# Unread identity matmuls in three waits of TensorE, and a constant in place of a computed wait before expert 0's later tiles

## The reference

```python
h = layernorm(x) * (1 + ca) + sa
xn = rms_scale * h / (norm(h) * D**-0.5 + 1e-8) * split_scale
K = sigmoid(xn @ W_K)
u, g_in, g_out = split(xn @ W_ugg, 3)
u = u * sigmoid(g_in) * (1 - K)
outputs = scan(a * prev + b, a=Kshift, b=u)        # along the sequence
x = x + ga * (outputs * sigmoid(g_out) @ W_out + h)
h = layernorm(x) * (1 + cb) + sb
# each token goes to 2 of 8 experts, with weights w
x = x + gb * sum_e w_e * (gelu(h @ W1[e] + b1[e]) @ W2[e] + b2[e])
```

## Time and profile before

| what | value |
|---|---|
| time, median of 3 runs | 755.43 us (754.45 to 755.51) |
| profiled execution: span, first to last instruction | 770.2 us |
| its time over the span | not given apart from the span |
| TensorE busy | 705.5 us, 92% of the span |
| VectorE, ScalarE, POOL busy | 517.6, 416.1, 393.3 us |
| mean granted TensorE clock | 0.956 of full speed |
| opening, up to the first main product | 24.15 us |
| main stage | last logits of group 6 at 288.3 us |
| expert stage, from its first product | 312.24 us |

### The profile page before, as it was taken

One profiled execution on the slowest core, in us unless ns is written; L12 is line 12 of the kernel. 1 busy time (PEld: TensorE's weight loads), 2 busy tenths in 40 slices (PEclk: granted clock), 3 DMA queues, 4 the chain that ended last, 5 costly groups with the idle time before them and its releaser, 6 DMA issues.

```text
span 770.2 us, 16815 instructions
## 1 busy us (share of the span) xinstructions
PE 705.5 (92%) x4854; PEld 651.0 (85%) x4854; DVE 517.6 (67%) x1788; ACT 416.1 (54%) x1082; POOL 393.3 (51%) x309
## 2 busy tenths in 40 slices
PE   5899999999999993489998999999998999999991
PEld 1678888788888873389998999999898999999991
DVE  5878879998887668375553754647866476476451
ACT  5456564655546351165654755547665575475560
POOL 1264637785683654633534635446555445463443
PEclk9799999999999995589999999999999999999996
DMA  8441012230110413414457344555553553433432
GB/s 300 146 160 56 1 55 71 83 112 29 56 55 31 153 69 106 152 40 73 62 111 175 61 73 64 121 132 166 124 114 63 123 130 91 100 62 63 74 70 37
DMA packets 50308, 72.54 MB, mean 94 GB/s; under 512 B 5808, under 2 KB 42108, under 8 KB 50240
## 3 DMA queue, kind: packets, MB, share of 16 engines
q0 software_dynamic: 16480, 27.28, 19.4%
q1 hardware_dynamic: 33760, 44.46, 18.4%
HBM read 48.85 MB, written 22.87 MB: 93 GB/s over the span
## 4 chain that ended last, share of the span: by engine, by line
PE 76%; DVE 9%; issue 6%; DMA 4%; ACT 2%; POOL 2%; SPq 0%; DVEq 0%; another core or an unknown queue 0%; POOLq 0%; ACTq 0%
PE mm L965 24%; PE yb L976 23%; PE mm L810 17%; PE yb L835 5%; PE tp L944 2%; DMA out_x<-ysb,tokb 2%; PE tp L866 1%; PE tp L825 1%; PE tp L853 1%; DVE hl L1330 1%; ACT xnb L651 1%; DMA mb<-mod_rows 1%; DMA gbr<-mod_rows,xm 1%; DVE bst L1011 1%; DMA h2all<-in_L_wmod 1%
## 5 line engine op out<-in xcount | busy, mean ns | idle before, releaser
L783 ACT ACTIVATE hh<-mm,b1T 128x256 fp32r<-128x256 f32 (+1 forms) x288 | 135.9, 472 | 174.5 <-PE mm L965 124.5
L576 POOL DMA_INDIRECT out_x<-ysb,tokb x68 | 109.2, 1606 | 187.2 <-DVE ysb L1359 147.0
L1330 DVE TENSOR_TENSOR hl<-mm,hh 128x256 fp32r<-128x256 f32 (+1 forms) x288 | 116.3, 407 | 128.5 <-ACT mm L784 115.3
L965 PE MATMUL mm<-fh,SH 128*128 128x256 f32 x576 | 166.4, 289 | 22.7 <-DVE hl L1330 8.4
L965 PE MATMUL mm<-fl,SH 128*128 128x256 f32 x576 | 163.3, 283 | 0.0
L965 PE MATMUL mm<-fh,SL 128*128 128x256 f32 x576 | 162.9, 283 | 0.0
L976 PE MATMUL yb<-SH,hh 128*128 128x256 f32 x544 | 156.9, 288 | 0.0
L976 PE MATMUL yb<-SH,hl 128*128 128x256 f32 x544 | 153.6, 282 | 0.0
L976 PE MATMUL yb<-SL,hh 128*128 128x256 f32 x544 | 153.5, 282 | 0.0
L965 PEld LDWEIGHTS mm<-fh,SH 128*128 128x128 f32 x576 | 110.7, 192 | 26.5 <-DVE hl L1330 10.3
L784 ACT ACTIVATE mm<-mm,b1T 128x256 f32<-128x256 f32 (+1 forms) x288 | 127.5, 443 | 0.0
(11 more groups left out here) (218 smaller groups left out, 1172.8 us busy)
## 6 DMA issues: line engine op xcount, KB each, us to landing
xin<-disp_x SPq DMA_DIRECT2D x74, 132.0 KB
wraw<-in_L_ffn_W SPq DMA_DIRECT2D x8, 1024.0 KB
h2all<-in_L_ffn_W SPq DMA_DIRECT2D x8, 1024.0 KB
xb<-in_L_attn_x SPq DMA_DIRECT2D x8, 512.0 KB, 7.5
out_x<-x2b SPq DMA_DIRECT2D x8, 512.0 KB
mb<-mod_rows SPq DMA_DIRECT2D x3, 768.0 KB, 6.4
wraw<-in_L_attn_W_ugg SPq DMA_DIRECT2D x1, 1536.0 KB, 10.2
gbr<-mod_rows,xm POOLq DMA_INDIRECT x74
```

Of the source, the lines that this page charges most:

```text
L576: e.indirect_dma_start(out=out_rows, out_offset=bass.IndirectOffsetOnAxis(ap=tokb[:, j:j + 1], axis=0), in_=ysb[:, j, :], in_offset=None, ...
L783: e.activation(hh[:, f, c_], mm[f % 4][:, c_], ACT.Gelu_apprx_tanh, bias=bias)
L965: i = e.matmul(mm[f % 4][:, 0:TE], a[:, k, f * 128:(f + 1) * 128], b[:, k, :], start=(k == 0 and t == 0), stop=(k == 1 and t == 2))
L1330: e.tensor_tensor(hl[:, f, w_], mm[f % 4][:, w_], hh[:, f, w_].bitcast(F32), ALU.subtract)\
```

## The change

TensorE's program gets a helper, `keep_busy(n)`: n matmuls of `ident` by `ident` (128 by 128, fp32) into 128 columns of `yb[1]`, which nobody reads. Six are issued as soon as `ident` is made, three after the transpose of `vrow`, 28 after the mod products and before the transposes of group 0. On ScalarE `ln1_square(0)` moves ahead of `mod_rows(0)`. On SP `wait_for_groups` and the registers that it uses are taken out; in its place SP waits for `SENT_8` once, between expert 0's first tile and its later ones, and the wait for `SENT_8` behind those tiles goes.

```diff
--- before.py
+++ after.py
@@ -359,12 +359,9 @@
                 for j in range(2):
                     e.dma_start(xin[:, j, :], rows_of(j)).then_inc(S["rows_loaded"], 16)
 
-            r_late, r_soon, r_sooner, r_sent = (e.alloc_register("sp_" + k) for k in ("late", "soon", "sooner", "sent"))
+            r_late = e.alloc_register("sp_late")
             e.wait_ge(S["late_ready"], 1)
             e.reg_load(r_late, lateint[0:1, 0:1])
-            e.reg_load(r_soon, lateint[0:1, 1:2])
-            e.reg_alu(r_soon, r_soon, 1, ALU.logical_shift_left)
-            e.reg_add(r_sooner, r_soon, 1)
             e.reg_mov(r_last, CAP - 128)
             e.wait_ge(S["sent0"], 16 * 8 * 4)
             e.wait_ge(S["sent1"], SENT_6)
@@ -388,22 +385,7 @@
                     e.reg_add(r_pos, r_pos, 128)
                     return Xd[bass.ds(e.snap(r_at, min_val=0, max_val=E * CAP - 128), 128), :]
 
-                def wait_for_groups():
-
-                    e.reg_add(r_sent, r_pos, TE)
-                    e.reg_alu(r_sent, r_sent, 1, ALU.logical_shift_left)
-                    e.reg_alu(r_sent, r_sent, r_soon, ALU.max)
-                    e.reg_alu(r_sent, r_sent, r_sooner, ALU.min)
-                    e.reg_alu(r_sent, r_sent, 1, ALU.bitwise_and)
-                    e.reg_alu(r_sent, r_sent, 8, ALU.logical_shift_left)
-                    e.reg_add(r_sent, r_sent, SENT_6)
-                    e.reg_alu(r_sent, r_sent, SENT_6, ALU.max)
-                    e.wait_ge(S["sent1"], r_sent)
-                    e.sem_inc(S["tick_sp"], 1)
-
                 def tile(first, parts):
-                    if n == 0 and not first:
-                        wait_for_groups()
                     load(rows_of)
                     if first and n == 0:
                         e.wait_ge(S["x2_scaled"], NG)
@@ -420,8 +402,8 @@
                 if n == 0:
                     tile(True, 2)
                     ks = counts_of(e)
+                    e.wait_ge(S["sent1"], SENT_8)
                     more_tiles(e, ks, n, tile)
-                    e.wait_ge(S["sent1"], SENT_8)
                     load_b2(1, E)
                 else:
                     tiles(e, ks, n, tile)
@@ -711,8 +693,8 @@
             ln1_scale(0)
             weights_high(0, 0)
             weights_high(0, 1)
+            ln1_square(0)
             mod_rows(0)
-            ln1_square(0)
             weights_high(1, 0)
             weights_high(1, 1)
             ln1_xn(0)
@@ -883,9 +865,16 @@
                 e.matmul(o, ones[:, :], bc(csum[:, :], 4), start=False, stop=True,
                          skip_group_check=True).then_inc(S["ranked"], 1)
 
+            def keep_busy(n):
+
+                for _ in range(n):
+                    e.matmul(yb[1][:, 0:128], ident[:, :], ident[:, :], start=True, stop=True)
+
             e.wait_ge(S["const_made"], 6)
+            keep_busy(6)
             e.wait_ge(S["vec_loaded"], 64)
             e.transpose(tp[0][:, 0:76], vrow[:, :], ident[0:76, 0:76]).then_inc(S["vec_turned"], 1)
+            keep_busy(3)
             e.wait_ge(S["c_silu"], 1)
             e.wait_ge(S["wmod_loaded"], 16)
             for to, c0 in ((mm[3], D), (yb[0], 0)):
@@ -900,6 +889,7 @@
                     i = e.matmul(mm[n][0:NB, :], scT[:, k, :], wmod_sb[:, k, n * 512:(n + 1) * 512],
                                  start=(k == 0), stop=(k == 1))
                 i.then_inc(S["mod_made"], 1)
+            keep_busy(28)
             turn_xn(0)
             for g in range(NG):
                 last = g == NG - 1
```

## The result

The changed kernel takes 758.84 us (median of 14 runs), the kernel before 755.30 in runs beside it: a ratio of 1.0045, interval 1.0029 to 1.0060. It is slower by 0.45%, 3.4 us. The forecast was 755.0, no change, in a range up to 757.5.

The account below looks back on a forecast made before the run. TensorE was taken to bound the kernel, but group 1's normalized rows, behind the mod-row chain, to gate the opening. Opening -0.4 us, constant wait 0: 755.4 - 0.4 = 755.0 us, range 752.6 to 757.5.

Parts of the forecast that it names:

- the constant wait: 0: SP's load of expert 0's second tile: wait over by 327.8 at worst, 8 us before the need; cost 0.
- Rival E: Expert 0's second tile: needed at 328.4, its rows arrive 324.5 to 330.8; 0 to 2.4 us lost; chance 0.10.
- the 0.58 for no change: Whole kernel: the chance given to a measured time within 0.2% of the kernel before.
- The opening: Up to group 1: the guards' chain starts 0.4 us earlier and everything behind group 1 moves with it; -0.4 us.
- keep_busy(6) and (3): Opening, TensorE: 12 passes of 2.6 us and 6 of 1.3 us fit before DMA waits end; cost nothing.
- the 56 passes: keep_busy(28) behind the mod products: 0.116 us each, 6.5 us in all, from 14.4 to 20.9.
- The block's overrun: keep_busy(28) ends at 20.9, the rows to be turned are ready at 20.77: overrun 0.1 us.
- Rival C: Opening: clock rises late, keep_busy(28) ends at 23.7, group 0's transposes start 2.9 us late; 757.6; chance 0.16.
- Rivals B: Opening: mod-row chain shorter in timed runs, so TensorE gates and its saved 2.7 us go through; 752.3; chance 0.18.
- D: New TensorE idle before 49.5: clock falls, 3.25 us at the lower level cost 1.6 us; 756.6; chance 0.08.
- one time for the rise: Opening: TensorE's clock reaches its upper level near 7.9, as work begins at 2.1 and 5.8 us precede the rise.

Follow-up runs that it names:

- e1: Kernel before, its computed wait written as a branch around a constant wait; old opening: 754.94 us, ratio 1.0005 to the kernel before.
- e2: e1 plus the change's lines on TensorE and ScalarE (new opening, computed wait): 755.45 us, ratio 1.0001 to the kernel before.
- e3: Kernel before with only the change's SP lines (constant wait ahead of tile 2, old opening): 758.50 us, ratio 1.0061.
- e4: As e3, but the constant wait stands behind the load of each later tile of expert 0: 756.09 us, ratio 1.0016 to the kernel before.
- e5: e1 with the first gating of W_out moved from POOL to VectorE behind its first scan: 755.62 us, ratio 1.0017 to the kernel before.
- e9: e1 (old opening, computed wait) with POOL's first gather of gate rows ahead of its last four sends: 752.38 us, ratio 0.9956 to the kernel before.
- e6: e2 with the first gating of W_out moved from POOL to VectorE behind its first scan: 757.27 us, ratio 1.0030 to the kernel before.
- e8: Changed kernel (constant wait) with POOL's first gather of gate rows ahead of its last four sends: 760.08 us, ratio 1.0090 to the kernel before.
- e7: e2 with POOL's first gather of gate rows ahead of its last four sends: 751.29 us, ratio 0.9966 to the kernel before.
- e11: e7 with 14 instead of 28 idle matmuls ahead of group 0's transposes: 752.37 us, ratio 0.9970 to the kernel before.
- e12: e7 with 44 instead of 28 idle matmuls ahead of group 0's transposes: 756.01 us, ratio 1.0016 to the kernel before.
- e10: e9 with only the swap of squares and mod_rows on ScalarE: 751.72 us, ratio 0.9963 to the kernel before.

## Why the prediction was wrong

**The step that failed** is "the constant wait: 0". It took the need for tile 2's rows from one row, 335.89, and SP's present issue from another, 327.62, and found 8 us of slack. Both rows came from an execution that had been held up by 14 us between tiles 1 and 2. Without that, the need is at 318 to 319 and the issue at 313.5 to 313.9 (e1, e2). The release of the wait was well bounded (0 to 6.4 us after POOL's last send; measured 2.9, and SP's load followed at 322.03). Set against a need at 318, it gives a wait of TensorE of 3 us at the least; measured were 7.6, since the load takes 3.5 more from its issue to the transposes. The price was 0.61%, 4.6 us (e3).

**Rival E** was this mechanism, and its end was short: 0 to 2.4 us. It put the need at 335.89 - 7.44, taking out one idle of TensorE that had a row, although SP's load had been late in the same execution, and although the prediction itself noted 14.8 us between span and median. Those 14.8 were short too, since a time is 1.7 us longer than its span. Taking all of them out at this place would have put the need near 321, and the wait, by the prediction's own 324.5 to 330.8 for the rows, at 3.4 us or more. The chance of 0.10 was the wrong one, and with it the 0.58 for no change.

**The opening**, -0.4 us: the mechanism held, step by step. keep_busy(6) and (3) fitted their gaps; the mod products ended at 14.57 (forecast 14.4), the 56 passes at 21.03 (20.9) with 0.116 us each, so the row was right and the 0.081 us that the Trainium skill, TensorE: Matmul & The Clock Gate, section Back-to-back issue gap, gives for a matmul of 128 columns isn't reached by these fp32 passes; main products began at 23.47 (23.7). The block's overrun was 0.4 us (rows complete at 20.40, transposes from 20.86) where 0.1 was forecast. The 2.4 us that TensorE saved became idle at the first scan and before group 1's transposes, as said. Those were at 49.10, not 49.8, but the five other profiles of the old opening (e1, e3, e4, e5, e9) had them at 49.00 to 49.59: 50.22 was a late one. The changed kernel, e2 and e7 had them at 48.95 to 49.10, so the new opening gains between nothing and 0.6 us where its block doesn't overrun, and the times of e2 and e1 can't tell that from nothing.

**Rival C**, the overrun, had a chance of 0.16 as a state of all executions. The runs show it as a share of them: two of the five profiles that have the new opening with 28 (e6 and e8; not after, e2 and e7).

**Rivals B and D** did not come. TensorE's 2.7 us did not go through to group 1, and group 1's transposes after the idle of 1.1 us took 1.09 us, as in the earlier trace rows: the upper level.

**Left open:** why SP's register instructions and TensorE were slow in the profiled execution of the kernel before (no other profile's span is above 756.3), where the early gather gains its time, and the rest of e3's price: of its 4.6 us tile 3's transposes show 2.0 to 2.5, and the whole spans of e3's and e1's profiles 2.9 (756.0 and 753.1).

## What to carry to other kernels

A wait made simpler must be priced against when its data is needed in a normal execution: compare the profile's span with the median first, and where they differ, find the stretch that holds the difference before taking any slack from it. A constant wait for "all sends" ends only when POOL has been through its whole queue of sends, here 2.9 us after the last one; what else is put into that queue ahead of them lengthens it. A fixed block of filler work must be short enough to end in time also when it starts at its latest: once issued, it runs to its end.

## What the runs showed that was not expected

The same opening with the same 18 unread passes ahead met its first products at either level of the clock: the four passes from 7 on took 1.10 us in the changed kernel's profile, e2 and e7, and 1.99 to 2.04 us in e6 (from 8.85), e8, e11 and e12. The forecast took one time for the rise, 7.9 from one profile, and neither group is at it. In e8, e11 and e12 the products ended at 16.2 to 16.4, no sooner than in three profiles of the old opening without any unread matmul (e3, e4, e5: 15.8 to 16.0). So in these three the 18 passes ahead did not bring that end forward.

The idle that TensorE had left at the upper level in the new opening (1.6 us ahead of the main products, 1.3 and 1.1 later) was followed by the lower level in none of these profiles, though in the earlier trace rows an idle of 2.27 us had been. In the old opening an idle of 3.58 us ahead of the transposes was followed by it. In e10, an old opening, the transposes took 1.09 us after an idle of 4.11 us, the upper level, and only the main products behind them stepped by 0.43, the lower. e11, with 14 unread matmuls in that idle, had its main products step by 0.23 us, the upper level.
